# ScalarE's order inside an expert tile: the copy of the high rows ahead of the SiLU in every tile

## What is computed

```python
def ffn(x):                                   # 8 experts, the best 2 for each row, D = 512, H = 352
    scores = xf @ gate_w.T + gate_b + bias
    top_scores, top_idx = jax.lax.top_k(scores, 2)
    gates = jax.nn.softmax(top_scores, axis=-1)
    comb = jnp.sum(jax.nn.one_hot(top_idx, E) * gates[..., None], axis=1)
    h = jax.nn.silu(jnp.einsum('td,ehd->teh', xf, w1) + b1)
    y = jnp.einsum('teh,edh->ted', h, w2) + b2
    return jnp.einsum('ted,te->td', y, comb)

x = x + 0.5 * ffn(layernorm(x))
x = x + attention(layernorm(x))               # projections, convolution, scan over time, output projection
x = x + 0.5 * ffn(layernorm(x))
```

## Time and profile before

| | |
|---|---|
| time, median of 3 runs | 881.02 us (879.1 to 882.88) |
| the profiled execution's own time | 880.63 us |
| its span, first to last instruction | 878.9 us |
| TensorE busy | 756.0 us (86%) |
| VectorE busy | 611.2 us (70%) |
| ScalarE busy | 358.6 us (41%) |
| GpSimd busy | 229.5 us (26%) |
| mean granted TensorE clock | 0.933 of full speed |

### The profile page before, as it was taken

How to read it: one execution, slowest core, us unless ns; L and a number is a source line. 1 busy time by engine, 2 the same in 40 slices (tenths; PEclk the granted TensorE clock), 3 DMA queues, 4 the chain that set the end, 5 groups by cost and what they waited for, 6 DMA issues and landing times.

```text
span 878.9 us, 13888 instructions
## 1 busy us (share of the span) xinstructions
PE 756.0 (86%) x4182; PEld 413.8 (47%) x4183; DVE 611.2 (70%) x1006; ACT 358.6 (41%) x623; POOL 229.5 (26%) x224
## 2 busy tenths in 40 slices
PE   8689899999972998997999999999529999999910
PEld 5346465556641444443444444445226666666600
DVE  6876556666644569999989989995775555555546
ACT  5856234334323436455544654532703332333200
POOL 3113544544521002001211101021113444444300
PEclk9899999999995998998999999999859999999965
DMA  9963648875518401700531302354736733333269
GB/s 325 395 240 138 258 154 332 304 257 161 186 72 238 97 1 48 144 0 21 100 60 13 66 7 46 143 132 135 317 104 234 256 115 109 118 113 113 91 224 378
DMA packets 45242, 137.26 MB, mean 156 GB/s; under 512 B 5776, under 2 KB 5776, under 8 KB 41872
## 3 DMA queue, kind: packets, MB, share of 16 engines
q1 hardware_dynamic: 27824, 86.38, 27.2%
q0 software_dynamic: 17376, 50.34, 20.6%
HBM read 85.32 MB, written 51.38 MB: 156 GB/s over the span
## 4 chain that ended last, share of the span: by engine, by line
PE 71%; DVE 13%; DMA 6%; ACT 3%; issue 3%; SPq 1%; POOL 1%; DVEq 0%; POOLq 0%; ACTq 0%
PE bank L628 59%; PE bank L622 5%; PE bank L721 3%; DMA space<-xn_rows,slot_src 2%; DMA space<-y_rows 2%; PE bank L847 2%; PE bank L671 1%; DVE space L1548 1%; DVE space L1545 1%; DVE space L1338 1%; SPq L487 1%; DVE bst L1329 1%; DMA space<-x_in 1%; DMA y_rows<-space,slot_dst 1%; PE bank L781 1%
## 5 line engine op out<-in xcount | busy, mean ns | idle before, releaser
L628 PE MATMUL bank<-space 128*128 (+3 forms) x2958 | 580.9, 349 | 23.0 <-DVE space L1399 12.8
L628 PEld LDWEIGHTS bank<-space 128*128 128x128 f16 (+1 forms) x2958 | 273.0, 99 | 276.8 <-issue 30.7
L554 POOL DMA_INDIRECT y_rows<-space,slot_dst x78 | 85.8, 1100 | 159.1 <-DVE space L1459 158.5
L550 POOL DMA_INDIRECT space<-xn_rows,slot_src x78 | 81.7, 1047 | 126.0 <-PE bank L622 67.2
L1440 DVE TENSOR_TENSOR space<-bank,space 128x512 f16<-128x512 f32 x78 | 53.9, 691 | 82.7 <-ACT space L1027 82.7
L1032 ACT ACTIVATE space<-space 128x352 f32<-128x352 f32 x78 | 38.7, 496 | 154.5 <-DVE space L1446 154.5
L1446 DVE SCALAR_TENSOR_TENSOR space<-bank,space 128x352 f32<-128x352 f32 x78 | 40.9, 524 | 66.0 <-PE bank L628 63.5
L622 PE MATMUL bank<-ident,space 128*128 128x128 f32 x440 | 67.7, 284 | 11.7 <-DMA space<-xn_rows,slot_src 9.9
L1459 DVE TENSOR_SCALAR space<-bank,slot_gate 128x512 f32<-128x512 f32 x78 | 58.5, 750 | 18.6 <-PE bank L628 16.3
L1037 ACT ACTIVATE space<-bank 128x384 f16<-128x384 f32 x78 | 38.2, 489 | 71.5 <-PE bank L721 71.4
L1545 DVE SCALAR_TENSOR_TENSOR space<-space,cang 128x512 f32<-128x512 f32 x84 | 63.0, 751 | 5.5 <-ACT space L1118 3.3
(11 more groups left out here) (181 smaller groups left out, 737.6 us busy)
## 6 DMA issues: line engine op xcount, KB each, us to landing
space<-ffn_w SPq DMA_DIRECT2D x8, 1472.0 KB, 10.0
w_saved<-space SPq DMA_DIRECT2D x8, 1472.0 KB
space<-w_saved SPq DMA_DIRECT2D x8, 1472.0 KB, 8.7
xn_rows<-space SPq DMA_DIRECT2D x8, 1024.0 KB, 6.8
space<-y_rows SPq DMA_DIRECT2D x32, 256.0 KB, 6.4
space<-x_in SPq DMA_DIRECT2D x7, 1024.0 KB, 8.3
space<-att_w SPq DMA_DIRECT2D x12, 518.0 KB, 4.0
space<-y_rows POOLq DMA_DIRECT2D x6, 1024.0 KB, 9.2
```

Source lines behind the costliest of these rows:

```text
L550: gp.indirect_dma_start(dst, None, rows, bass.IndirectOffsetOnAxis(ap=index, axis=0)).then_inc(done, 16)
L554: gp.indirect_dma_start(y_rows, bass.IndirectOffsetOnAxis(ap=slot_dst[:, t:t + 1], axis=0), yo[:, t % 2], None).then_inc(y_st[t % 2], 16)
L628: last = pe.matmul(dst, a, b, start=(n == 0), stop=(n == len(terms) - 1))
```

## The change

ScalarE's `step` takes the order of `first_step`, and `first_step` goes. `x_high(t + 2)` stands ahead of `silu(t + 1)` in every tile. No instruction is added or removed on any engine, and no wait changes; only ScalarE's order does, in steps 8 to 36 of the first stage and 0 to 36 of the second.

```diff
                 def step(t, par):
                     h_high(t, par)
-                    silu(t + 1, 1 - par)
-                    x_high(t + 2, par)
-
-                def first_step(t, par):
-                    h_high(t, par)
                     x_high(t + 2, par)
                     silu(t + 1, 1 - par)
...
                 silu(0, 0)
                 x_high(1, 1)
                 for t in range(2 * PEELED):
-                    if ph:
-                        step(t, t % 2)
-                    else:
-                        first_step(t, t % 2)
+                    step(t, t % 2)
                     if not ph and t < E - OWN - BYPE:
                         split_high(OWN + BYPE + t)
```

## The result

The changed kernel takes 876.11 us (median of 9 runs, 875.13 to 879.61), the kernel before 881.52 us in the same comparison (9 runs). The ratio is 0.9943, with an interval of 0.9927 to 0.9960: by the ratio 5.0 us less (the two medians alone are 5.4 apart), where the prediction had 6.7. It lies inside the stated range and on the stated side.

What follows compares the result with a forecast made beforehand. TensorE was taken to wait for `x_low`, behind a ScalarE copy queued after the SiLU. Gains of 4.3 + 0.35 + 0.6 + 1.6 = 6.85 us, rounded to 6.7, gave 874.3 us (ratio 0.992), range 870.8 to 878.2.

Steps and rivals of the forecast that it cites:

- The bound: Second-stage loop: `up` starts 0.14 us behind `x_low`, so TensorE waits for it; matmuls alone don't set the pace.
- Second stage, 4.3 us: Tiles 1 to 37: period from 4.625 to 4.50 us, 4.5 us less 0.2 held back for late tiles; range 3.4 to 4.7.
- The cover, 0.76 us: Time from the SiLU's end to the next `ht`; it hides the SiLU's 0.05 us later start behind the copy.
- Tiles 23 to 33, 0.6 us: First stage, pieces without stores: ten tiles take 46.25 us instead of 46.83, gain 0.6 us (0.3 to 0.9).
- Tiles 9 to 23, 1.6 us: First stage, pieces and stores: 14 periods gain 0.055 + 0.06 us each, 1.6 us in all (0.7 to 2.3).
- Tiles 33 to 37, 0.35 us: First stage, tiles without pieces: four periods gain 0.09 us each, 0.35 us in all.
- may meet TensorE's clock at another moment: Earlier starts of attention and the second stage may meet another clock moment; the 6.85 us sum was rounded to 6.7.
- TensorE is the bound after all: Rival, chance 0.13: loops have their own TensorE pace near 4.62 us; gain 0 to 3 us, taken as 880.
- slower: Rival, chance 0.05: the SiLU, queued behind the copy, arrives last and delays `ht`; 885.6 us if 1.0 us later.
- Rival 3: Chance 0.10: first stage's piece tiles stay at 4.76, heavy stretch at 4.79; it yields 0.5 us, second stage 4.3: 876.2.

Runs made afterwards that it cites:

- second_only: Kernel before with the new ScalarE order in the second stage alone, first stage in its old orders: 878.01 us, ratio 0.9948.
- delay: Changed kernel with none to three extra ScalarE copies between `x_high` and the SiLU in the second stage's written-out steps: 877.69 us in one execution.
- no_loads: new_piece with TensorE using expert 0's weights in the first stage's loop steps, not loading the expert number there: 872.33 us, ratio 0.9892.
- new_piece: Changed kernel with the piece's conversion moved: ScalarE between a pair's steps, VectorE between `h_low` and `add_bias` of the second tile: ratio 0.9917.
- first_only: Kernel before with the new ScalarE order in the first stage alone: 880.71 us, ratio 0.9982.
- hoist: new_piece with stores in the last eight turns and TensorE's middle expert-number load at the pair's top, ahead of `ht`: 877.71 us, ratio 0.9961.

## Why the prediction was right, and which terms were off

- **The bound.** "TensorE is waiting for `x_low`, for a little in each second tile": right. The second stage went from 4.625 to 4.50 us a tile when the copy was moved, and `x_low` is 0.75 us early. The gap of 0.14 us from `x_low` to `up` stood in both tiles of the pair, not in each second one alone (in the tile before, `x_low` ends at 716.58 and `up` starts at 716.72).
- **Second stage, 4.3 us.** Measured 4.20 in second_only and 3.40 in the profiled execution of the changed kernel. The step and its size were right; the 0.2 us held back "for single tiles" was too little for an execution in which a gather is late (0.8 us).
- **The cover, 0.76 us.** Right in kind, 0.66 by delay. The 0.05 us by which the SiLU is later costs nothing.
- **Tiles 23 to 33, 0.6 us.** This term failed: nothing was gained (-0.21). Two of its readings were carried over from other kinds of tiles. The first is that `y_out` "then comes 0.20 us after `ht`", from a step that is written out. It stayed at 0.29, `down` at 2.82, and the chain over the piece kept its whole length. The second, and larger one, is the 1.94 us from `down` to the next `ht`, from the second stage. In the tiles with a piece it was 1.95 to 2.07 us before and is 1.95 to 2.14 after the change, 2.04 on average. With 2.82 and 2.04 a tile with a piece takes 4.86 us, where the term had 4.72. The range of the term (0.3 to 0.9) should have had the zero in it: its own text says that this chain hangs "not on ScalarE".
- **Tiles 9 to 23, 1.6 us.** Mis-sized: 1.08. "Half of it as a wait for `x_low`" was a split between two unknowns. From `down` to `ht` it stayed at 2.0 to 2.2 us instead of 1.94, and by the trace its source is TensorE's load of the expert number, which no_loads shows for new_piece; it was in the trace of before, under the transposes' "issue", and I didn't open it.
- **Tiles 33 to 37, 0.35 us.** Measured 0.07. Two of the four tiles went to 4.50 us. The tile at the loop's end, 35, takes 4.74 (4.69 before), held by the three loads behind the loop, and tile 36 stays at 4.55.
- **The sum.** It came out inside the range because the second stage, two thirds of it, was right. The three terms of the first stage had 2.55 us, and 0.94 was measured (0.82 in first_only).
- **The rest.** The stretches give 4.3 us in the profiled execution, which was 3.1 faster; the ratio gives 5.0. Between the stages the executions differ by more than that difference: from tile 37 of the first stage to tile 0 of the second it is 409.1 us in the trace of before and 411.0 in that of the changed kernel, with 408.4 to 411.5 in the others. A part of it is visible at the start of attention, in the granted clock (the columns are those of the busy times above, the clock is the third number from the end). Before:

```profile
282.00:289.00 7.00, 5.57 (x18) 1.78 (x17) 0.00 (x0) 3.14 (x6) 1.31 (x1) 0.74 0.62 105
```

and after:

```profile
282.00:289.00 7.00, 6.05 (x17) 1.91 (x16) 0.00 (x0) 2.08 (x4) 1.31 (x1) 0.50 0.56 85
```

The changed kernel came to its attention 1.5 us earlier, ran these 7 us at the lower of the two clock levels all through (0.50), and in the next 7 us both were near full clock (0.98 and 0.99). Of its lead of 1.5 us, 0.4 was left at 290 us. Another 0.6 us went just ahead of the second stage's tile 0, where TensorE is idle with "issue" twice, for 0.24 and 0.28 us; the cause of that is open. That an earlier start "may meet TensorE's clock at another moment" was in the prediction; whether it will cost or help in a given execution these runs don't settle.

The rival "TensorE is the bound after all" fell with 4.50 us in a loop; "slower" with delay. Rival 3, the pieces' chain and a heavy stretch that keeps its pace, was nearest to what happened in the first stage (0.5 us there, 0.8 to 0.9 measured), and its 876.2 is nearest to the median of 876.1; I gave it 0.10. The forecast's own 874.3 is 1.6 us too low by its first-stage terms.

## What to carry to other kernels

In a kernel whose engines each have a fixed order, read the starts: if one instruction starts at a constant short distance (here 0.14 us) behind the end of another, tile after tile, that one sets the pace, however full the busy times look. Then ask what stands ahead of it in its queue without being needed; putting the copy that VectorE and then TensorE wait for ahead of a SiLU with 0.7 us of slack was worth 0.6% here and cost nothing. A saving at one place holds only where no other chain closes as soon: check each kind of tile for it (with a piece, with a store, in a loop, written out) before multiplying by the count.

## What the runs showed of the hardware

- A load of one number from memory on the chip into an engine's register took 0.30 to 0.58 us in the second stage, and up to 1.42 us (changed kernel) and 1.78 us (new_piece) in the stretch with stores of 1472 KB. What followed a late load on TensorE started 0.34 to 0.49 us behind its end, and the wait shows as "issue" there. In 14 tiles of new_piece it cost 4.2 us (68.02 less 63.78).
- Halving the store did not shorten such a load: 1.78 us at most with 736 KB as with 1472 KB, and nine tiles were late instead of six.
- Two transfers of 1472 KB that start 1.6 us apart made a gather late enough to cost 3.5 us in the eight tiles around them (38.13 against 34.59 us; without the new order 4.5 us, 39.09 against 34.58).
- With the two loads of a pair in a row ahead of `ht`, every second tile in the loop of hoist's second stage takes 0.25 to 0.40 us more than 4.50, and the others 0.05.
